# Neighbour max over a graph: who copies the vacant row, and who waits for the far gathers

## The reference

```python
vals, idx = jax.lax.top_k(jnp.where(A != 0, -arange(N), -inf), 25)
feats = jnp.where((vals > -inf)[..., None], x[idx], -inf)
agg = feats.max(axis=2)
agg = jnp.where((degree <= 25)[..., None], jnp.maximum(agg, 0.0), agg)
out = relu(concat([x, agg], -1) @ W + b)
return layernorm(x + out)
```

## Time and profile before

| | us |
|---|---|
| median of 3 runs (2535.0 to 2538.99) | 2536.08 |
| the profiled execution | 2534.37 |
| its span, first to last instruction | 2532.6 |
| VectorE busy | 2242.7 (89%) |
| ScalarE busy | 1935.1 (76%) |
| GpSimd busy | 1884.9 (74%) |
| TensorE busy | 2133.9 (84%) |
| mean granted TensorE clock | 0.967 of full |

### The profile page before, as it was taken

How to read it: one execution, slowest core, us unless ns; L and a number is a source line. 1 busy time by engine, 2 the same in 40 slices (tenths; PEclk the granted TensorE clock), 3 DMA queues, 4 the chain that set the end, 5 groups by cost and what they waited for, 6 DMA issues and landing times.

```text
span 2532.6 us, 48263 instructions
## 1 busy us (share of the span) xinstructions
PE 2133.9 (84%) x12832; PEld 1619.5 (64%) x12832; DVE 2242.7 (89%) x4815; ACT 1935.1 (76%) x3314; POOL 1884.9 (74%) x1861
## 2 busy tenths in 40 slices
PE   4888788778887898889888988868888898888986
PEld 3666566656665666666666666646666666666764
DVE  3999899989988999999998999989999999988996
ACT  7877688667775787888787887858878788877862
POOL 4777777777767777777776777777777777777776
PEclk7999999999998999999999999989999999999998
DMA  5445444553345334443344433464334443344421
GB/s 176 142 137 120 116 123 150 134 117 112 124 142 127 118 120 127 147 138 119 115 133 137 136 117 113 140 134 138 119 108 140 146 123 120 109 137 128 120 75 44
DMA packets 202576, 317.98 MB, mean 126 GB/s; under 512 B 59966, under 2 KB 85962, under 8 KB 202178
## 3 DMA queue, kind: packets, MB, share of 16 engines
q1 hardware_dynamic: 120002, 199.23, 24.0%
q0 software_dynamic: 82176, 114.59, 18.5%
HBM read 405.28 MB, written 16.78 MB: 167 GB/s over the span
## 4 chain that ended last, share of the span: by engine, by line
DMA 29%; issue 29%; POOL 20%; DVE 15%; PE 3%; POOLq 2%; ACT 1%; DVEq 1%; SPq 0%; ACTq 0%
DMA got<-in_x,index 29%; POOL got L457 18%; DVE nearest L843 3%; DVE hot L829 2%; POOL got_more L452 2%; PE near_ps L725 2%; DVE got L974 1%; DVE got L977 1%; DVE got L961 1%; DVE key_left L876 1%; POOLq L465 0%; DVE word_top L878 0%; DVE word_top L874 0%; DVE got L979 0%; PE out_ps L745 0%
## 5 line engine op out<-in xcount | busy, mean ns | idle before, releaser
L457 POOL DMA_INDIRECT got<-in_x,index x1664 | 1824.8, 1097 | 612.0 <-issue 468.1
L725 PE MATMUL near_ps<-heads,hot 128*128 128x256 f32 x5920 | 1442.3, 391 | 333.5 <-DVE nearest L843 308.9
L725 PEld LDWEIGHTS near_ps<-heads,hot 128*128 128x128 f32 x5920 | 1115.6, 194 | 594.2 <-DVE nearest L843 382.6
L843 DVE TENSOR_TENSOR nearest<-near_ps,nearest 128x1024 f32<-128x1024 f32 (+2 forms) x632 | 748.1, 1184 | 82.1 <-ACT flag L501 32.7
L572 ACT ACTIVATE got<-ones_col 128x3328 f32<-128x3328 f32 x128 | 380.9, 2976 | 0.0
L536 ACT ACTIVATE val<-z_ps,rank_col 128x1024 f16<-128x1024 f32 (+1 forms) x256 | 228.2, 891 | 158.6 <-PE z_ps L692 158.2
L829 DVE TENSOR_SCALAR hot<-val 127x128 f32<-127x128 f16 (+7 forms) x896 | 281.2, 386 | 0.0
L555 ACT ACTIVATE far<-val,beyond 128x128 bf16<-128x128 f16 (+7 forms) x488 | 253.6, 589 | 0.1
L541 ACT ACTIVATE mask_t<-adj_sb 128x2048 bf16<-128x2048 int32 x128 | 243.4, 1901 | 0.0
L545 ACT ACTIVATE mask_t<-mask_t 128x2048 bf16<-128x2048 bf16 x128 | 242.4, 1894 | 0.0
L567 ACT ACTIVATE nearest<-near_ps 128x1024 f32<-128x1024 f32 x128 | 130.9, 1022 | 143.6 <-PE near_ps L725 143.5
(11 more groups left out here) (126 smaller groups left out, 2178.1 us busy)
## 6 DMA issues: line engine op xcount, KB each, us to landing
adj_sb<-in_adj_turned SPq DMA_DIRECT2D x512, 256.0 KB
xx_sb<-in_x_both SPq DMA_DIRECT2D x128, 256.0 KB
got<-in_x,index POOLq DMA_INDIRECT x1664
out<-y SPq DMA_DIRECT2D x128, 128.0 KB
heads<-in_x_near SPq DMA_DIRECT2D x32, 384.0 KB, 3.9
hot<-vacant SPq DMA_DIRECT2D x80, 12.0 KB
got_more<-in_x,index_more POOLq DMA_INDIRECT x48, 5.6
w_sb<-in_L_gnn_W SPq DMA_DIRECT2D x1, 512.0 KB, 9.1
```

The source lines that it names most:

```text
L457: pool.indirect_dma_start(out=to, out_offset=None, in_=x_rows, in_offset=bass.IndirectOffsetOnAxis(ap=at, axis=0), bounds_check=a.g * (N + ...
L725: mm = pe.matmul(near_ps[:, buffer_of(a, k), s - k * ROUND:s - k * ROUND + 1, :], hot[:, a.i, s * P:(s + 1) * P], heads[:, a.side, c, None ...
L843: dve.tensor_tensor(nearest[:, a.i, 0:n, :], near_ps[:, buffer_of(a, k), 0:n, :], nearest[:, a.i, 0:n, :], ALU.max).then_inc(near_taken, 1)
```

## The change

ScalarE issues the copy of the vacant row, right after `take_sign` and ahead of its wait for the small sums. At the end of its step SyncE waits for the landings of gathers 9 to 12 of a2, one after the other (each wait is followed by an increment of `rows_seen`), and then increments `rows_in` once. VectorE waits for `rows_in` in `combine_early`, in place of the four landings there; its waits in `combine_late` and in `combine_more` go. So `combine_early` now waits for all 13 gathers of its tile.

```diff
@@ SyncE's step
-                if now.there:
-                    b = Tile(pair, u, 0)
-                    sp.wait_ge(vacant_ready, done(now.T))
-                    sp.sem_inc(vacant_begun, 1)
-                    if b.there:
-                        sp.wait_ge(near_taken, taken(b.g, b.t, ROUNDS[b.t] - 1))
-                    sp.dma_start(hot[P - 1:P, now.i, 0:NEAR[now.t] * P].rearrange("o (s n) -> o s n", n=P),
-                                 vacant[0:NEAR[now.t], now.q, :]).then_inc(vacant_in[now.i], 16)
...
                     load_adj(ahead, 3)
+                if now.there:
+                    for s in range(FAR - UNDER_WAY, FAR):
+                        sp.wait_ge(*landed_of(now, s))
+                        sp.sem_inc(rows_seen, 1)
+                    sp.sem_inc(rows_in, 1)
@@ ScalarE
+            def place_vacant(a, before):
+                act.wait_ge(vacant_ready, done(a.T))
+                act.sem_inc(vacant_begun, 1)
+                if before.there:
+                    act.wait_ge(near_taken, taken(before.g, before.t, ROUNDS[before.t] - 1))
+                act.dma_start(hot[P - 1:P, a.i, 0:NEAR[a.t] * P].rearrange("o (s n) -> o s n", n=P),
+                              vacant[0:NEAR[a.t], a.q, :]).then_inc(vacant_in[a.i], 16)
...
                     take_sign(next)
+                if a2.there:
+                    place_vacant(a2, a0)
@@ VectorE, combine_more
-                for s in range(FAR - UNDER_WAY, FAR):
-                    dve.wait_ge(*landed_of(a, s))
-                dve.sem_inc(rows_in_branch, 1)
@@ VectorE, combine_early
-                for s in range(EARLY - UNDER_WAY, EARLY):
-                    dve.wait_ge(*landed_of(a, s))
-                dve.sem_inc(rows_at_vec, 1)
+                dve.wait_ge(rows_in, done(a.T))
@@ VectorE, combine_late
-                for s in range(FAR - UNDER_WAY, FAR):
-                    dve.wait_ge(*landed_of(a, s))
-                dve.sem_inc(late_at_vec, 1)
```

More of the change, by code:

```diff
@@ L226, in build @@
         flag_by_pool = sem("flag_by_pool")
-        rows_at_vec = sem("rows_at_vec")
-        late_at_vec = sem("late_at_vec")
-        rows_in_branch = sem("rows_in_branch")
         more_at_vec = sem("more_at_vec")
@@ L234, in build @@
         more_gathered = sem("more_gathered")
+        rows_seen = sem("rows_seen")
+        rows_in = sem("rows_in")
         landed = [sem(f"landed{place}") for place in range(UNDER_WAY)]
@@ L372, in _ @@
                 sp.sem_inc(stored[i], 16)
+            sp.sem_inc(rows_in, BASE)
             for piece in range(PIECES):
```

## The result

The changed kernel takes 2521.05 us (median of 5 runs, 2519.95 to 2522.99), the kernel before beside it 2536.08 (5 runs, 2534.06 to 2539.21): ratio 0.9941, 95% interval 0.9929 to 0.9952. It is faster by 0.6%, and the forecast was 2521. The profiled execution is the one of 2521.05 us, with a span of 2519.3: 13.3 us shorter than the profiled span before.

What follows compares the result with a forecast made beforehand. VectorE narrowly paces GpSimd in the loop; GpSimd paces itself in the last pair. -18.4 + 1 + 2.65 = -14.8 from the profiled 2534.37 gives 2519.6, plus 1.71 to the median: 2521 us, range 2510 to 2542 (forecast's own 2514 to 2530).

Steps and rivals of the forecast that it cites:

- Saving in the loop: 22.4 us: VectorE before the early combine: idle time falls from 37.9 us to 0.16 each over 97 tiles (bounds 34.6 and 0).
- more saved: Rival: idle time before the early combine near 0.034 us, all GpSimd slack used, -24.8 us, so 2511; chance 0.08.
- I deduct 4 us, 18.4 us reach the border: Loop: 4 us of the 22.4 lost where GpSimd is behind its index; 18.4 reach the border near 1960 us.
- The last pair, +1: Straight code of the last two graphs: 1 us added for bursts of VectorE that fall worse under the new wait.
- The tail, +2.65: Last tile: early combine's two instructions now follow the last landing, 2.49 us, plus 0.03 and 0.13 for the relay.
- the relay's 0.13: Last tile: passing the landing to VectorE through SyncE costs about 0.13 us (bounds 0 and 0.5).
- The copy, 0: Vacant row's copy moved from SyncE to ScalarE: costs 0 under ScalarE's idle time, and gains 0 in the last pair.
- L501's wait unchanged: ScalarE's wait ahead of L501, 159.0 us over 92 waits in the loop, was to stay unchanged.
- Gathers held more often: Rival: L961's shift slows the loop's gathers by 27.5 ns each, 35.3 us, eating GpSimd's slack: 2547; chance 0.16.
- The lock rule: By it an earlier L961 stands behind the running gather, losing the 18.4 us (2540); chance 0.04 shared with late signal.

Runs made afterwards that it cites:

- e1_swap: Kernel before, with VectorE's four landing waits in combine_early put ahead of its wait for the last near round: 2511.13 us, ratio 0.9911.
- e8_half: Kernel before, with two of the four landing waits ahead of the near-round wait and two behind it: 2524.46 us, ratio 0.9952.
- e7_self_collect: Changed kernel, with VectorE itself waiting for gathers 9 to 12 behind its near-round wait, instead of SyncE's signal: 2538.95 us, ratio 1.0013 to the kernel before.
- e4_early8: Changed kernel, with a second SyncE signal so the early combine waits for eight gathers and the late one for all: 2515.22 us, ratio 0.993 to the kernel before.
- e2_copy_only: Kernel before, with only the copy of the vacant row moved to ScalarE's queue: 2536.25 us, ratio 1.0007.
- e3_copy_back: Changed kernel, with the copy of the vacant row back on SyncE's queue: 2519.14 us, ratio 0.9949 to the kernel before.
- e6_no_early_hold: Kernel before with landing waits ahead of the near-round wait, the early combine's two maxima replaced by one-input reductions (maxima left out): 2485.12 us, ratio 0.9798.
- e9_swap_and_copy: Kernel before, with the four landing waits ahead of the near-round wait and the vacant row copied by ScalarE: 2513.75 us, ratio 0.9914.

## Why the prediction was right

The time was met, in part by two errors of opposite sign: more idle time went than I said, and less of it reached the end. That it agrees to the microsecond is luck. The sum was -14.8 us against the profiled execution before; between the two profiled spans it is -13.3. The 1.7 us that I added to get from that execution to the median make up the rest, because the profiled execution of the changed kernel is its median.

- **The mechanism was right.** Idle time before the early combine is the issue of waits: e1_swap and e8_half take it away, whole and half, by the place of the waits alone, and e7_self_collect brings it back by four waits in the old place.
- **"Saving in the loop: 22.4 us" was mis-sized: 34.4.** I took 0.16 us for two waits left behind the near round. None was left there: the idle time fell to 0.036, the end that I had called the rival "more saved". I counted how many waits there were; what counted was which ones come behind the one that ends last. That such a wait could pass beneath the near round was in my own text, where the late combine's waits cost nothing for that reason.
- **"I deduct 4 us, 18.4 us reach the border" was wrong in kind: 15.6 of 34.4.** I gave the stretches in which GpSimd is behind its index a gain of zero. In the first of them it lost 4.7 us, 4.2 of it on gathers held by the combines, and the overflow branch passed it on to VectorE (+7.3 us idle there over four tiles). Another 8.5 us came back as waits before the near rounds. GpSimd's index waits fell from 40.9 to 31.1, not to 20. Up to the start of tile 97's early combine VectorE's idle time fell by 19.4 in all and its busy time rose by 3.8 (1735.55 to 1739.39), which makes the 15.6 of the border. Why the busy time rose isn't shown.
- **"More saved, all slack used: 2511"** gave the time of e1_swap, 2511.13, though not by its steps: there too GpSimd keeps 31 index waits, 21.3 us, and the price at the end isn't paid (14.7 us from the last gather to the end).
- **The last pair, +1: measured -0.5.** VectorE does wait for SyncE's signal, 11 times and 21.8 us in all, and GpSimd doesn't notice, as said. The burst that I priced at 1 us was not there.
- **The tail, +2.65: measured +2.8**, and 17.17 - 14.70 = 2.5 against e4_early8. The late combine of the last tile starts 2.4 us after the landing (1.39 after 2502.14), not 2.6: the relay's 0.13 was nothing.
- **The copy, 0:** held in three pairs of kernels. No wait of TensorE for the vacant row is left. "L501's wait unchanged" was wrong: it fell from 159.0 to 137.2, and to 138.0 in e1_swap, where the copy stays on SyncE, so this comes with the earlier combine. A wait that I had not seen came up in the last pair: ScalarE waits 17.7 us for adjacency rows, 9 times. It goes with the copy's place and not with SyncE's new waits, since e2_copy_only has it (15.8 us) and e3_copy_back, which has the new waits, does not. By the time of e2_copy_only it costs nothing that can be told.
- **Gathers held more often:** the mean moved from 1084 to 1082 in the loop and from 1139 to 1148 behind it, within the 10 ns that I had allowed. My reason for it was wrong, though. Gathers that begin inside the early combine lost 47.1 us in the loop (37.4 before), those inside the late one 26.1 (39.2 before): the phase did change, and the two nearly cancelled.
- **The lock rule:** L963 starts earlier and takes at most 1.281 us in 128 (1.276 before). In no kernel of the study does an early combine take over 1.30 us, so it isn't blocked by a running gather. The other half of the rule in the Trainium skill, SBUF — State Buffer, "Who interferes with whom", agrees with the runs: a VectorE instruction with two SBUF inputs contends with a GpSimd instruction that reads SBUF, one with a single SBUF input, outside the 2-port perf modes, does not (1.92 us for the gather at 1209.47 in the changed kernel, 1.00 for that at 1200.88 in e6_no_early_hold).

**What stays open.** Why e1_swap ends 9.9 us before the changed kernel (7.6 by the ratios), where I expected 3. In the profiles 2.5 us are the tail, 5.0 lie in the loop (border 1945.1 for 1950.1) and 1.9 in the last pair. The copy is none of it (e9_swap_and_copy). In the loop the changed kernel idles 67.1 us before its near rounds and e3_copy_back 66.9, e1_swap 64.0 and e9_swap_and_copy 62.3; the signal from SyncE is what differs, but no run shows by what path it would cost that. Part may be the phase between gathers and combines alone: the mean gather in the loop ranges from 1080 to 1093 ns over the kernels with unchanged combines, and 10 ns x 1284 are 13 us of GpSimd's time.

## What to carry to other kernels

Put the waits that are already met ahead of the one that ends last; in a loop with computed thresholds each one left behind it delays the instruction by some 0.09 us, and moving them takes no other engine. Before you count such a saving, look at each stretch for the engine that paces it, and allow it a loss where another engine's timing slows it, not only a gain of zero. Where two engines meet in a fixed rhythm, look at where they meet: here one combine moved back by 0.35 us in 30 tiles took the time from 0.9911 to 0.9879 of before.

## What was not expected of the hardware

- A gather that begins inside a VectorE maximum with both inputs in SBUF, more than some 40 ns behind its start, ends no sooner than 0.86 us after that instruction ends: the gather at 1209.47 ends at 1211.39, L963 at 1210.52, though L966 (two inputs as well) begins at 1210.55. The gather alone takes 1.00 us, so one that begins in the last tenth of a microsecond of the maximum shows nothing.
- The one-hot columns, which read one tile of SBUF in 16 bits, hold gathers too, in another way: in 92 tiles of the changed kernel a gather that begins up to 0.5 us before the first and longest of these instructions (0.95 us) ends 0.12 us after it. The gather at 1235.92 takes 1.30 us, and the one-hot instruction begins at 1236.14. That is 34 us of gather time in all, and no run here tried to take it away.
- The hold fixes the rhythm behind it: the next gathers start at 1211.69 and 1212.99, and the late combine of that tile starts at 1212.99 too. A few hundredths decide whether it holds another one for 0.9 us. In the straight code, where it comes 0.16 us sooner behind the early combine (3.54 us for 3.70), it holds one in 29 of 31 tiles, in the changed kernel and in e1_swap.
- Waiting costs VectorE by the place: 0.036 us between two instructions with the register waits passed beforehand, 0.21 with two of them behind, 0.39 with four, 0.19 for four waits on constants (one of those 31 is still the loop's code, with 0.41; without it 0.18).
